# Dealing the next step's matrix products one behind each tile in a selective state-space stage

## The reference

```python
xz = x @ in_w.T
xh, z = jnp.split(xz, 2, axis=-1)
xc = silu(conv_b + sum(xp[:, k:k + L, :] * conv_w[:, k] for k in range(4)))   # xp: xh padded by 3
proj = xc @ xproj_w.T                       # dt (16), B (16), C (16)
delta = softplus(dt @ dt_w.T + dt_b)
h = exp(delta * A) * h + (delta * xc) * B   # for every token, channel and state
y = (h * C).sum(over states) + xc * D_param
y = (y * silu(z)) @ out_w.T
```

## Time and profile before

| | us |
|---|---|
| median of three runs | 4086.89 |
| lowest and highest | 4086.31, 4087.93 |
| profiled execution | 4088.45 |
| its span | 4086.5 |
| PE busy | 3684.2 (90%) |
| DVE busy | 2935.9 (72%) |
| ACT busy | 2759.7 (68%) |
| POOL busy | 1443.8 (35%) |

### The profile page before, as it was taken

The page is one execution under the profiler, slowest core; times in us unless marked ns, Lnnn a source line. Parts: engine busy times, 40 slices in busy tenths (PEclk is TensorE's granted clock), DMA queues, the critical chain, the costliest instruction groups (busy, mean ns, idle before and its releaser), DMA issues. The chain is left out here.

```text
span 4086.5 us, 64166 instructions
## 1 busy us (share of the span) xinstructions
PE 3684.2 (90%) x20577; PEld 1992.2 (49%) x20577; DVE 2935.9 (72%) x3944; ACT 2759.7 (68%) x3830; POOL 1443.8 (35%) x1284
## 2 busy tenths in 40 slices
PE   7799999999999999658988889898888989887899
PEld 4223333233323332235666666666666666666454
DVE  5799999899989997144777777777777777777121
ACT  2256766667666667416888888788878888887232
POOL 3000000000000000003777666777766777777000
PEclk9789999999999999778999999999999999999899
DMA  5510100101010100140111111111111111112321
GB/s 141 142 34 3 41 18 26 32 12 40 4 40 4 40 4 4 64 138 32 43 53 53 48 47 53 42 63 53 53 42 53 53 42 53 48 48 64 114 77 61
DMA packets 121702, 202.32 MB, mean 50 GB/s; under 512 B 25392, under 2 KB 68368, under 8 KB 121456
## 3 DMA queue, kind: packets, MB, share of 16 engines
q1 hardware_dynamic: 101264, 173.97, 13.2%
q10 hardware_dynamic: 18656, 20.85, 1.7%
q0 software_dynamic: 1536, 4.20, 0.7%
HBM read 147.83 MB, written 50.72 MB: 49 GB/s over the span
## 5 line engine op out<-in xcount | busy, mean ns | idle before, releaser
L1047 POOL TENSOR_TENSOR m_g<-m_hs,m_cb 128x512 f32<-128x512 f32 x1024 | 1287.8, 1279 | 530.1 <-DVE m_hs L1323 519.6
L661 DVE TENSOR_REDUCE a_mx<-a_ps_m 128x1 f32<-128x512 f32 x2048 | 1311.1, 685 | 156.9 <-PE a_ps_m L520 139.3
L632 ACT ACTIVATE a_probs<-a_ps_s 128x1024 f32<-128x1024 f32 x1024 | 995.0, 1020 | 466.3 <-PE a_ps_s L557 465.7
L1323 DVE TENSOR_TENSOR_SCAN m_hs<-m_da,m_carry,m_ps_x 128x512 f32<-128x512 f32 x768 | 949.1, 1268 | 332.1 <-PE m_ps_x L1120 326.7
L1249 ACT ACTIVATE m_da<-m_delta,m_a_cur 128x512 f32<-128x512 f32 x1024 | 731.7, 715 | 182.5 <-DVE m_hs L1323 181.6
L520 PE MATMUL a_ps_m<-a_k,a_q 112*128 112x512 bf16 x2048 | 732.0, 394 | 41.6 <-DMA a_q<-q_scr 26.3
L1120 PE MATMUL m_ps_x<-m_ident,m_bu 128*128 128x128 f32 x4096 | 646.6, 282 | 98.6 <-DVE m_hs L1323 77.9
L1234 ACT ACTIVATE m_bu<-m_dut,m_bt 128x512 f32<-128x512 f32 x1024 | 730.0, 713 | 2.3 <-PE m_ps_x L1120 2.1
L1132 PE MATMUL m_ps_y<-m_ident,m_g 128*128 128x128 f32 x4096 | 629.5, 277 | 14.4 <-POOL m_g L1047 14.1
L1120 PEld LDWEIGHTS m_ps_x<-m_ident,m_bu 128*128 128x128 f32 x4096 | 477.4, 145 | 299.0 <-issue 212.4
L557 PE MATMUL a_ps_s<-a_q,a_k 115*128 115x512 bf16 (+1 forms) x2048 | 611.3, 381 | 1.4
(11 more groups left out here) (156 smaller groups left out, 2559.3 us busy)
## 6 DMA issues: line engine op xcount, KB each, us to landing
m_cb<-c_scr SPq DMA_DIRECT2D x128, 512.0 KB, 3.6
y_scr<-m_ysb SPq DMA_DIRECT2D x16, 1024.0 KB, 4.2
ffn_y<-y_scr SPq DMA_DIRECT2D x16, 1024.0 KB, 10.2
a_k<-k_scr SPq DMA_DIRECT2D x224, 64.0 KB, 2.2
a_q<-q_scr SPq DMA_DIRECT2D x224, 64.0 KB, 2.6
m_xn<-xn_scr SPq DMA_DIRECT2D x16, 512.0 KB, 4.9
q_scr<-p_partsq SPq DMA_DIRECT2D x24, 256.0 KB, 2.4
k_scr<-p_partsk SPq DMA_DIRECT2D x24, 256.0 KB
```

What stands on the lines that cost most here:

```text
L632: nc.scalar.activation(probs[:, t % 2, 2 * half:2 * half + 2], ps_s[half][:, :, :], ACT.Exp, scale=float(DK) ** -0.5).then_inc(exped, 1)
L661: nc.vector.reduce_max(mx[:, i // NC, i % NC:i % NC + 1], bank(i), AX.X).then_inc(m_maxed, 1)
L1047: nc.gpsimd.tensor_tensor(g[:, t % NG], hs[:, t % NHS], cb[:, quarter % 2, n % CQ], ALU.mult).then_inc(g_ok, 1)
L1323: nc.vector.tensor_tensor_scan(hs[:, t % NHS, rev], da[:, t % NDA, rev], ps_x[:, t % NX, rev], carry[:, n, i:i + 1] if p else 0.0, ALU.mul ...
```

## The change

- The order of the fills changes: `PROJ`, `BT` and `DELTA` come before `YT`; `Z`'s last three fills come after `DUT`.
- `fill` takes a part: `XH`, `CONV`, `PROJ` and `Z` are issued one product at a time, one part behind each tile from `PE_FROM` on; the halo's products stay with the last part of `CONV`, whose taps run in the opposite order. Each fill still waits once, before its first part, and signals once, with its last.
- y's transposes move from tiles 20 to 24 to tiles 44 to 47, their takes from 23 to 28 to 48 to 51.
- ACT's `SILU` moves from 24 to 27, `PROJ`'s take from 31 to 35 and `BT`'s from 34 to 37. The first softplus moves from 38 to 39 and its joins stay at 37 and 38; the second moves from 46 to 45 and its joins from 45 and 46 to 43 and 44. du is formed behind tile 44 instead of 46.
- The skip goes behind the additions of state 5 instead of state 1.
- On SP c's store moves behind the load of pair 6 instead of 4, y's store to the end of a step's loads; the loads of the inputs wait for the new last fill of `Z`.

The core of the diff:

```diff
@@ mamba()
-        order = [(u, j) for u in range(STEPS + 2) for j in range(FILLS)
+        sequence = [*range(XH, YT), *range(PROJ, Z), *range(YT, PROJ), Z, *range(DUT, DUT + NTB), *range(Z + 1, DUT)]
+        order = [(u, j) for u in range(STEPS + 2) for j in sequence
...
-        PE_AT = {1: XH, 3: XH + 1, 5: XH + 2, 7: XH + 3,
-                 9: CONV, 12: CONV + 1, 15: CONV + 2, 18: CONV + 3,
-                 20: YT, 21: YT + 1, 23: YT + 2, 24: YT + 3,
-                 27: PROJ, 30: BT, 31: DELTA, 33: DELTA + 1, 40: DELTA + 2, 41: DELTA + 3,
-                 48: Z, 49: Z + 1, 51: Z + 2, 52: Z + 3,
-                 54: DUT, 55: DUT + 1, 57: DUT + 2, 58: DUT + 3}
+        parts = {j: KD if j < CONV or Z <= j < DUT else DC if j < YT else ND if j == PROJ else 1 for j in sequence}
+        PE_FROM = {0: XH, 2: XH + 1, 4: XH + 2, 6: XH + 3,
+                   8: CONV, 12: CONV + 1, 16: CONV + 2, 20: CONV + 3,
+                   28: PROJ, 33: BT, 34: DELTA, 35: DELTA + 1, 40: DELTA + 2, 41: DELTA + 3,
+                   44: YT, 45: YT + 1, 46: YT + 2, 47: YT + 3, 48: Z,
+                   50: DUT, 51: DUT + 1, 52: DUT + 2, 53: DUT + 3, 54: Z + 1, 56: Z + 2, 58: Z + 3}
+        PE_AT = {k + part: (j, part) for k, j in PE_FROM.items() for part in range(parts[j])}
+        SKIP_AT = 5
...
         ACT_AT = {5: XH, 7: XH + 1, 9: XH + 2, 11: XH + 3,
-                  23: YT, 24: SILU, 25: YT + 1, 26: YT + 2, 28: YT + 3,
-                  31: PROJ, 34: BT, 38: SOFTPLUS, 46: SOFTPLUS + 1,
-                  52: Z, 53: Z + 1, 55: Z + 2, 56: Z + 3,
-                  57: DUT, 58: DUT + 1, 60: DUT + 2, 61: DUT + 3}
+                  27: SILU, 35: PROJ, 37: BT, 39: SOFTPLUS, 45: SOFTPLUS + 1,
+                  48: YT, 49: YT + 1, 50: YT + 2, 51: YT + 3, 53: Z,
+                  54: DUT, 55: DUT + 1, 56: DUT + 2, 57: DUT + 3, 59: Z + 1, 61: Z + 2, 63: Z + 3}
...
-        DVE_AT = {11: CONV, 14: CONV + 1, 17: CONV + 2, 20: CONV + 3,
-                  32: DELTA, 33: DELTA + 1, 37: JOIN, 38: JOIN + 1,
-                  41: DELTA + 2, 42: DELTA + 3, 45: JOIN + 2, 46: JOIN + 3}
-        DU_AT = 46
+        DVE_AT = {11: CONV, 15: CONV + 1, 19: CONV + 2, 23: CONV + 3,
+                  34: DELTA, 35: DELTA + 1, 37: JOIN, 38: JOIN + 1,
+                  40: DELTA + 2, 41: DELTA + 3, 43: JOIN + 2, 44: JOIN + 3}
+        DU_AT = 44
...
@@ load_xn, load_win
-                        sp.wait_ge(filled, number[s - 2, Z + ND - 1] + 1)
+                        sp.wait_ge(filled, number[s - 2, Z + NTB - 1] + 1)
@@ SP's loop
                         load_c(s, h)
-                        if h == 4 and s > 0:
-                            store_y(s - 1)
-                        if h == 4 and s + 1 < STEPS:
+                        if h == 6 and s + 1 < STEPS:
                             store_c(s + 1)
+                    if s > 0:
+                        store_y(s - 1)
@@ fill (PE)
-                    if f >= NA:
+                    first, final = part == 0, part == parts[j] - 1
+                    if f >= NA and first:
                         evacuated(pe, f - NA)
...
-                        for k in range(KD):
-                            last = nc.tensor.matmul(bank, win[:, k, j * P:(j + 1) * P], xn[:, q, k], start=k == 0, stop=k == KD - 1)
+                        last = nc.tensor.matmul(bank, win[:, part, j * P:(j + 1) * P], xn[:, q, part], start=first, stop=final)
...
-                        pe.wait_ge(x_ok, s + 1)
-                        for k in range(ND):
-                            last = nc.tensor.matmul(bank[0:XPW], wxp[:, z, k], xc[:, q, k], start=k == 0, stop=k == ND - 1)
+                        if first:
+                            pe.wait_ge(x_ok, s + 1)
+                        last = nc.tensor.matmul(bank[0:XPW], wxp[:, z, part], xc[:, q, part], start=first, stop=final)
...
-                    last.then_inc(filled, 1)
+                    if final:
+                        last.then_inc(filled, 1)
@@ add (PE)
-                    if n == 1:
+                    if n == SKIP_AT:
@@ PE's loop
-                    if t < LAST and k in PE_AT and (s + 1, PE_AT[k]) in number:
-                        fill(s + 1, PE_AT[k])
+                    if t < LAST and k in PE_AT and (s + 1, PE_AT[k][0]) in number:
+                        fill(s + 1, *PE_AT[k])
```

More of the change, by code:

```diff
@@ L853 @@
 LAG = 4
-X_DT, X_B, X_C = 0, 32, 64
-XPW = X_C + DS
 CQ = 2
@@ L970, in load_win @@
                     if z:
-                        sp.wait_ge(filled, number[STEPS // 2 - 1, Z + ND - 1] + 1)
+                        sp.wait_ge(filled, number[STEPS // 2 - 1, Z + NTB - 1] + 1)
                     for half in range(2):
@@ L1052, in _, with fill @@
             def _(pe):
-                def fill(s, j):
+                def fill(s, j, part):
                     z, b, p, c = where(s if s < STEPS else 0)
@@ L1057, in fill @@
                     bank = ps_a[:, f % NA]
-                    if f >= NA:
+                    first, final = part == 0, part == parts[j] - 1
+                    if f >= NA and first:
                         evacuated(pe, f - NA)
                     if j < CONV:
-                        if j == XH:
+                        if j == XH and first:
                             pe.wait_ge(xn_in[q], 16 * (s // 2 + 1))
                             pe.wait_ge(win_in, 16 * 2 * (z + 1))
-                        for k in range(KD):
-                            last = nc.tensor.matmul(bank, win[:, k, j * P:(j + 1) * P], xn[:, q, k], start=k == 0, stop=k == KD - 1)
+                        last = nc.tensor.matmul(bank, win[:, part, j * P:(j + 1) * P], xn[:, q, part], start=first, stop=final)
                     elif Z <= j < DUT:
                         tb = j - Z
-                        for k in range(KD):
-                            last = nc.tensor.matmul(bank, xn[:, q, k, tb * P:(tb + 1) * P], win[:, k, DI:2 * DI], start=k == 0, stop=k == KD - 1)
+                        last = nc.tensor.matmul(bank, xn[:, q, part, tb * P:(tb + 1) * P], win[:, part, DI:2 * DI], start=first, stop=final)
                     elif YT <= j < PROJ:
@@ L1077, in fill @@
                         dt = j - CONV
-                        if dt == 0:
+                        if dt == 0 and first:
                             pe.wait_ge(taps_ok, 2 * z + 1)
                             pe.wait_ge(taken, takes[s, XH + ND - 1])
-                        nc.tensor.matmul(bank, taps[:, z, dt, DC - 1], xh[:, dt], start=True, stop=False)
-                        for tap in range(DC - 1):
-                            back = DC - 1 - tap
-                            here, there = (slice(0, CH - back), slice(back, CH)) if z else (slice(back, CH), slice(0, CH - back))
-                            last = nc.tensor.matmul(bank[:, here], taps[:, z, dt, tap], xh[:, dt, there],
-                                                    start=False, stop=p == 0 and tap == DC - 2)
-                        for tap in range(DC - 1 if p else 0):
+                        back = part
+                        here, there = (slice(0, CH - back), slice(back, CH)) if z else (slice(back, CH), slice(0, CH - back))
+                        last = nc.tensor.matmul(bank[:, here], taps[:, z, dt, DC - 1 - back], xh[:, dt, there],
+                                                start=first, stop=final and p == 0)
+                        for tap in range(DC - 1 if p and final else 0):
                             back = DC - 1 - tap
@@ L1143, in _ @@
                 pe.wait_ge(taps_ok, 2)
-                for j in range(FILLS):
+                for j in sequence:
                     if (0, j) in number:
-                        fill(0, j)
+                        for part in range(parts[j]):
+                            fill(0, j, part)
                 for t in range(LAST + LAG):
```

2 lines of the change are left out of this document (1 added, 1 removed).

## The result

The changed kernel takes 3943.25 us (median of four runs, 3942.12 to 3946.12) against 4087.41 for the kernel before, run on the same chip; the ratio is 0.9649, with a 95% interval of 0.9632 to 0.9665. The forecast was 3958. The profiled execution took 3942.12, its span 3940.3.

What follows compares the result with a forecast made beforehand. No engine is full throughout; the loss lies in waits moving between engines. A step gains 8.8 us, 123 over 14 steps; with 4 + 5 - 3 that is 129 off 4086.89: 3958, forecast 3935 to 3985 (68%), range 3928 to 4008.

Steps and rivals of the forecast that it cites:

- tiles 8-23: One product per tile and no skips keep PE full without pause: 37.62 us becomes 30.5, gain 7.1 a step.
- tiles 24-27: ACT's block waits for the fourth convolution's eviction, then runs 6.33 us: 13.11 becomes 7.8, gain 5.3 a step.
- tiles 28-35: ACT has no lead behind its block; PE stands some 2.1 us at tile 33 for the projection's take: loss 2.6.
- tiles 48-63: POOL forms du two tiles earlier, so PE waits 1.0 us for g at tile 49: loss 0.8 a step.
- step 0, last step, start: Step 0 gains 4 us, the last step 5 by losing its blocked transposes; Z's last three blocks cost 3 at the start.
- rival (c): A product alone between transposes costs 0.2 us more than one in a row, 6.2 a step: 4045; 4%.
- rival (d): The half clock sets in at PE's wait before tile 33's transposes and stays: slower, 4112 or so; 5%.
- the clock: PE's low clock at tile 24 should vanish, as no PE idle exceeds about 2.2 us; included in a 5.3 gain.
- Rival (e): Stretches with only transposes (tiles 36 to 47, 60 to 63) run at the half clock: 4092; 1%.
- (a): ACT has more lead and PE does not stand at tile 33: 2.5 us a step more, 3923; 8%.
- (b): Handovers taken as ties (joins at 37 and 43, y's takes, B's take) each slip, 3 us a step: 4000; 12%.
- (f): An unseen wait eats the gain in each step, 9 us: about 4085; 2%.

Runs made afterwards that it cites:

- late load: Against the changed kernel, ScalarE waits for VectorE's fourth convolution eviction first and only then loads its table, as the forecast had it: 4005.05 us.
- earlier take: Against the changed kernel, ScalarE's takes of the projection and of B's transposes each stand one tile earlier (34 and 36): 3930.00 us.
- three more kernels without that wait: The earlier take plus: last step's y takes at 46 to 49, 3923.74 us; those and two du products on VectorE, 3920.24; du's products dealt, 3928.02.
- the edit of that table alone: On top of the earlier take, ScalarE takes y at tiles 46 to 49 instead of 48 to 51 in the last step only: 3923.74 us.
- the skip at 1: The changed kernel with the skip put back behind the additions of state 1 (tiles 8 to 11): 4041.53 us.

## Why the prediction was right, and where it was not

The forecast said a gain of 129 us; 144 were measured, inside the range. Term by term, step 6 and the mean of steps 1 to 14:

| term | forecast | step 6 | mean |
|---|---|---|---|
| tiles 0-7 | +0.2 | +0.3 | +0.3 |
| tiles 8-23 | +7.1 | +7.2 | +7.0 |
| tiles 24-27 | +5.3 | +6.1 | +6.9 |
| tiles 28-35 | -2.6 | -2.0 | -2.4 |
| tiles 36-47 | -0.4 | -0.4 | -0.7 |
| tiles 48-63 | -0.8 | -0.6 | -0.8 |
| step | +8.8 | +10.6 | +10.3 |
| 14 steps | +123 | | +144.3 |
| step 0, last step, start | +4, +5, -3 | | +0.4, +0.8, -1.2 |

Right, by its mechanism: **tiles 8 to 23** as a sum of work on a full engine, to 0.1 us; rival (c) fell with it, since a lone product costs 0.86. **Tiles 48 to 63**: the wait for g at tile 49 is there, at 0.68 for my 1.0. **Tiles 28 to 35**: ScalarE without lead, PE standing at tile 33.

Mis-sized: **tiles 24 to 27.** The step that failed is the sentence that the block waits for the fourth eviction and then runs its 6.33. Its first 1.28, the table load, wait for nothing. Scan 28 came 9.4 after scan 23 instead of 10.3, the scan gap of 3 us that I named as a sign did not exist, and PE's wait at tile 33 was 0.60 instead of 2.1. The trace before had it already, in step 0, where the load begins ahead of the fourth eviction; in step 6 it only seemed to follow, since ScalarE's own exponential ended 0.05 behind the eviction (2642.72 and 2642.67):

```profile
1926.11 1.28 ACT L1193 ACT_TABLE_LOAD   x1
...
1926.61 0.72 DVE L1264 TENSOR_SCALAR m_xc<-m_ps_a,m_cols 128x512 f32<-128x512 f32 x1
```

The kernel with the late load is my schedule, and it shows what the error hid: its waits are where I put them (1.87), but the time is 4005, not 3961. At full clock my sum for it holds; what I rejected, with "1.96 did not, and mine is 2.1", was the half clock, which came in 11 of 15 steps. So one error made the forecast slow by 1.3 us a step (0.8 and 0.5), and the other would have made it some 45 us too fast had the wait really been as long as I put it. One row of step 0 was no evidence that a wait of that length is harmless; rival (d) deserved far more than 5%. That the total came out near the forecast is in part luck: the error on the load kept the wait short, and the skips in tiles 24 to 27, which I moved for another reason, hold PE back under it (2.18 without them).

The rest of the term's miss is the step that I took for all. Step 6 had 13.11 before, at 3.4 us of half clock; ten of the fourteen steps had 6.8 us, and the mean was 13.90.

Wrong: **the clock.** The low stretch left tile 24, as forecast, but 41.0 us of half clock remained elsewhere, a sign that I had named against myself. The earlier take shows that the wait of 0.60 at tile 33 draws most of it: 41.0 us against 6.8, and 3.4, 13.7 and 17.1 in three more kernels without that wait. The rule of the Trainium skill that I weighed (TensorE: Matmul & The Clock Gate, Part 4: PE-mode transpose) fares no better than before: tiles 36 to 47, transposes and two products of delta, ran at 1.00 in step 6, and tiles 60 to 63, transposes alone, kept the full clock in steps 1 to 14. Rival (e) did not come.

Wrong: **the last step and step 0.** I removed the blocked transposes from the last step in the sum, though their takes had only moved, to places 48 to 51, where ScalarE, with nothing else to do for a next step, comes late: 0.8 gained of 5, and the edit of that table alone brought 2.1. In step 0 tiles 8 to 23 gained 4.7 (PE waits for a take at tile 8 there) and tiles 48 to 63 lost 3.3, with a stretch of half clock at tile 49. For the start I had 3 lost; the first scan came 1.2 later, which tells nothing, since it lies anywhere from 1879.2 to 1888.7 in the kernels with the changed order.

**The other rivals.** (a) was half true: PE's wait at tile 33 was short. Its own time, 3923, lay under my range of 3928 to 4008, which I had said to hold most of it. (b) did not come; its ties slipped by 0.3 us a step in tiles 36 to 47, not by 3. No wait of the kind of (f) appeared.

**What stays open.** What decides whether one step keeps the full clock: steps with the same idle and the same work differ. The series ties the half clock of tiles 28 to 37 to PE's idle there, in kernels that differ in more than the idle; the earlier takes, the late load and the skip at 1 are edits of one line each. Why the 0.77 of the kernel before is harmless is not shown. The half clock at tile 41, in four steps of the changed kernel and one with the earlier take, stands behind a wait of 0.64 to 0.77 for VectorE, and so do the steps without it.

## What to carry to other kernels

Price an order by the idle time of the engine that is full, not by the gaps of the engine behind it: dealing four fills removed gaps of 2.8 us each on VectorE and gained 3 us in all. Before trusting a schedule whose full engine stops for 0.6 to 2 us once per round, ask what its clock does afterwards, over many rounds and not in one row; two takes moved by one tile were worth 13 us. And when a wait is moved in a table, follow it through the first and the last round, where the other entries of the table are empty.
